# Moving the moment arithmetic of both norms from VectorE to GpSimd

## What is computed

```python
x = x + _L0_conv_ref(_ln_c(x), ...)          # x: (16, 128, 28, 28); norm over the 128 channels of each pixel
t = _to_tokens(x)                            # 12544 tokens of 128 channels
t = t + _L0_ffn_ref(_ln_t(t), ...)           # norm over the channels again, 8 experts, 1024 tokens each

def _ln_c(v, eps=1e-06):
    m = jnp.mean(v, axis=1, keepdims=True)
    s = jnp.var(v, axis=1, keepdims=True)
    return (v - m) / jnp.sqrt(s + eps)
```

## Time and profile before

| what | us |
|---|---|
| median of 3 runs | 503.83 |
| lowest and highest run | 503.77, 505.05 |
| span of the profiled execution | 502.9 |
| busy in it: PE, DVE, ACT, POOL | 361.9, 327.1, 274.3, 159.3 |

### The profile page before, as it was taken

How to read it: one execution, slowest core, us unless ns; L and a number is a source line. 1 busy time by engine, 2 the same in 40 slices (tenths; PEclk the granted TensorE clock), 3 DMA queues, 4 the chain that set the end, 5 groups by cost and what they waited for, 6 DMA issues and landing times. The chain is left out here.

```text
span 502.9 us, 6936 instructions
## 1 busy us (share of the span) xinstructions
PE 361.9 (72%) x1947; PEld 255.7 (51%) x1947; DVE 327.1 (65%) x1004; ACT 274.3 (55%) x587; POOL 159.3 (32%) x151
## 2 busy tenths in 40 slices
PE   4989888888889985631021798999990498876575
PEld 3656555566666553520011374677560467464453
DVE  5699988888889898578879548556620025235444
ACT  3577888888888876677640528556551240510000
POOL 4000000000000000000005777787888788876000
PEclk9999999999999997655555799999997598997755
DMA  4604555555554342479101223344443267847998
GB/s 103 188 38 141 185 168 185 167 185 168 185 182 150 130 131 96 137 238 392 71 1 33 55 56 94 95 65 64 83 85 34 55 189 134 194 61 169 285 390 344
DMA packets 36396, 72.01 MB, mean 143 GB/s; under 512 B 6385, under 2 KB 16785, under 8 KB 36369
## 3 DMA queue, kind: packets, MB, share of 16 engines
q1 hardware_dynamic: 24256, 56.52, 35.0%
q0 software_dynamic: 9472, 8.66, 11.2%
q10 hardware_dynamic: 2640, 6.51, 3.3%
HBM read 34.96 MB, written 30.29 MB: 130 GB/s over the span
## 5 line engine op out<-in xcount | busy, mean ns | idle before, releaser
L403 POOL DMA_INDIRECT picked<-token_rows,slot_idx x32 | 31.5, 986 | 270.7 <-issue 270.4
L691 PE MATMUL psC<-x_pad,tap_diag 128*128 128x392 f32 x256 | 90.8, 498 | 6.7 <-ACT x_pad L570 5.6
L1009 DVE SCALAR_TENSOR_TENSOR conv<-x_pad,taps_w,conv 128x784 f32<-128x784 f32 x64 | 65.9, 1030 | 0.8
L691 PEld LDWEIGHTS psC<-x_pad,tap_diag 128*128 128x128 f32 x256 | 46.1, 189 | 37.0 <-DVE conv L1009 5.1
L1302 DVE TENSOR_TENSOR y_sum<-psC,b_rows 128x512 f32<-128x512 f32 x15 | 10.4, 692 | 75.2 <-PE psC L869 75.2
L869 PE MATMUL psC<-w,hid 128*128 128x128 f32 x480 | 56.6, 280 | 2.2 <-ACT hid L633 2.1
L869 PEld LDWEIGHTS psC<-w,hid 128*128 128x128 f32 x480 | 55.8, 197 | 4.6 <-issue 3.0
L613 ACT ACTIVATE picked_T<-psA 128x512 f32<-128x512 f32 x16 | 9.0, 594 | 59.9 <-PE psA L836 59.9
L426 POOL DMA_INDIRECT moe_sum_late<-y_rows,slot_idx x24 | 37.9, 1581 | 9.5 <-issue 7.0
L483 ACT ACTIVATE rows<-psD,sm 112x128 f32<-112x128 f32 x98 | 35.7, 464 | 9.3 <-DVE sm L1001 9.3
L729 PE MATMUL psB<-act,pw_masked 128*128 128x392 f32 x64 | 27.9, 563 | 17.0 <-DVE pw_masked L1085 17.0
(11 more groups left out here) (211 smaller groups left out, 728.8 us busy)
## 6 DMA issues: line engine op xcount, KB each, us to landing
token_rows<-rows SPq DMA_DIRECT2D x16, 416.5 KB, 3.6
x_in<-in_x_dram SPq DMA_DIRECT2D x16, 392.0 KB, 3.5
x_res<-in_x_dram SPq DMA_DIRECT2D x16, 392.0 KB, 4.3
moe_sum<-zero_rows SPq DMA_DIRECT2D x16, 392.0 KB, 4.9
x_all<-x SPq DMA_DIRECT2D x16, 392.0 KB, 2.9
moe_sum_late<-zero_rows SPq DMA_DIRECT2D x16, 392.0 KB, 7.7
out_dram<-act ACTq DMA_DIRECT2D x16, 392.0 KB, 6.2
w<-in_L_ffn_W_dram SPq DMA_DIRECT2D x16, 256.0 KB, 3.3
```

What stands on the lines that cost most here:

```text
L403: nc.gpsimd.indirect_dma_start(out=picked_in[k][:, b, :], out_offset=None, in_=rows_dram, in_offset=bass.IndirectOffsetOnAxis(ap=slot_idx[ ...
L691: ins = nc.tensor.matmul(psC[:, h, 0:HALF].rearrange("c (h w) -> c h w", w=W), tap_diag[:, n, :], x_pad_v[:, q, y0:y0 + LINES, dx:dx + W], ...
L1009: return nc.vector.scalar_tensor_tensor(o, x_pad_v[:, q, y0 + dy:y0 + dy + lines, dx:dx + W], taps_w[:, PE_TAPS + n:PE_TAPS + n + 1], acc, ...
```

## The change

The five DVE operations go. In their place POOL runs six small `tensor_tensor` operations on the same `st` and `sm`: difference, sum of squares and sum of means, then a square, a product with C/4 out of a small constant tile (`quarter`, set by one more memset), and the addition. Each of the last three waits for a semaphore that the one before it raises. POOL gets its own walk through the 22 steps. DVE's statistics wait for `moments` of the step before, since POOL must have read `st` first.

```diff
+            nc.gpsimd.memset(quarter[:, :], C / 4.0)
...
+            def moments(ln, row, number):
+
+                cols = columns(ln is not None, row is not None)
+                if ln is not None:
+                    pool.wait_ge(s_m1, ln + 1)
+                if row is not None:
+                    pool.wait_ge(s_m3, row + 1)
+                nc.gpsimd.tensor_tensor(sm[:, 1, cols], st[:, cols, 1], st[:, cols, 4], ALU.subtract)
+                nc.gpsimd.tensor_tensor(sm[:, 2, cols], st[:, cols, 2], st[:, cols, 5], ALU.add)
+                nc.gpsimd.tensor_tensor(sm[:, 0, cols], st[:, cols, 1], st[:, cols, 4], ALU.add).then_inc(s_ma, 1)
+                pool.wait_ge(s_ma, number + 1)
+                nc.gpsimd.tensor_tensor(sm[:, 1, cols], sm[:, 1, cols], sm[:, 1, cols], ALU.mult).then_inc(s_mb, 1)
+                pool.wait_ge(s_mb, number + 1)
+                nc.gpsimd.tensor_tensor(sm[:, 1, cols], sm[:, 1, cols], quarter[:, cols], ALU.mult).then_inc(s_mw, 1)
+                pool.wait_ge(s_mw, number + 1)
+                nc.gpsimd.tensor_tensor(sm[:, 3, cols], sm[:, 1, cols], sm[:, 2, cols], ALU.add).then_inc(s_mom, 1)
...
-            def stats(region, lo, s_math, img, s_turned):
+            def stats(region, lo, s_math, img, s_turned, done):
+                if since(done, 1):
+                    dve.wait_ge(s_mom, done)
...
                 if onN:
-                    stats(ln_region(imgN), 0, s_m1, imgN, s_t1)
-                    moments_a(new_ln, new_row, new)
-                    if not on1:
-                        moments_b(img0 + 1, new)
-                        moments_c(img0 + 1, new)
+                    stats(ln_region(imgN), 0, s_m1, imgN, s_t1, img0 + 1)
                 if on1:
                     first_tap(img1, q1, 0)
-                    if onN:
-                        moments_b(img0 + 1, new)
                 if on3:
                     keep_second()
-                if onN and on1:
-                    moments_c(img0 + 1, new)
                 if on3:
                     residual_sum()
                 if on4 and not onN:
-                    stats(row_region(img4), TPI, s_m3, img4, s_t3)
-                    moments_a(None, img4, new)
+                    stats(row_region(img4), TPI, s_m3, img4, s_t3, img0 + 1)
                 if on1:
                     first_tap(img1, q1, 1)
-                if on4 and not onN:
-                    moments_b(img0 + 1, new)
-                    moments_c(img0 + 1, new)
```

More of the change, by code:

```diff
@@ L142, in build @@
         st = sb("st", [P, 2 * TPI, 6])
+        quarter = sb("quarter", [P, 2 * TPI])
         sm = sb("sm", [P, 7, 2 * TPI])
@@ L214, in build, with columns @@
         row_tiles = psD[0:P, :, :].rearrange("p a (t c) -> p (a t) c", c=C)
+        def columns(on_ln, on_row):
+            return slice(0 if on_ln else TPI, 2 * TPI if on_row else TPI)
         def ln_region(img):
@@ L393, in _, with step @@
                            allow_small_or_imprecise_dtypes=True).then_inc(s_const, 1)
+            def moments(ln, row, number):
[13 more added lines that the diff above has]
+                nc.gpsimd.tensor_tensor(sm[:, 3, cols], sm[:, 1, cols], sm[:, 2, cols], ALU.add).then_inc(s_mom, 1)
+            def step(pair, u):
+                onN, imgN, _, _ = image(pair, u, -1)
+                on4, img4, _, _ = image(pair, u, 4)
+                if onN or on4:
+                    moments(imgN if onN else None, img4 if on4 else None, pair * 2 + u + 1)
+            moments(0, None, 0)
+            steps(pool, step)
             def gather(e, half):
@@ L965, in stats @@
                 ins.then_inc(s_math, 1)
-            def columns(on_ln, on_row):
-                return slice(0 if on_ln else TPI, 2 * TPI if on_row else TPI)
-            def moments_a(ln, row, cols):
-                if ln is not None:
-                    dve.wait_ge(s_m1, ln + 1)
-                if row is not None:
-                    dve.wait_ge(s_m3, row + 1)
-                nc.vector.tensor_tensor(sm[:, 1, cols], st[:, cols, 1], st[:, cols, 4], ALU.subtract)
-                nc.vector.tensor_tensor(sm[:, 2, cols], st[:, cols, 2], st[:, cols, 5], ALU.add)
-                nc.vector.tensor_tensor(sm[:, 0, cols], st[:, cols, 1], st[:, cols, 4], ALU.add).then_inc(s_ma, 1)
-            def moments_b(number, cols):
-                dve.wait_ge(s_ma, number + 1)
-                nc.vector.scalar_tensor_tensor(sm[:, 1, cols], sm[:, 1, cols], C / 4.0, sm[:, 1, cols], ALU.mult, ALU.mult)\
-                    .then_inc(s_mb, 1)
-            def moments_c(number, cols):
-                dve.wait_ge(s_mb, number + 1)
-                nc.vector.tensor_tensor(sm[:, 3, cols], sm[:, 1, cols], sm[:, 2, cols], ALU.add).then_inc(s_mom, 1)
             def inverse(ln, row, cols):
@@ L1089, in step @@
                 now_ln, now_row = img0 if on0 else None, img5 if on5 else None
-                new = columns(onN, on4)
-                new_ln, new_row = imgN if onN else None, img4 if on4 else None
                 def keep_second():
@@ L1157, in step @@
                 if on4 and not onN:
[L1158 to L1159 removed]
+                    stats(row_region(img4), TPI, s_m3, img4, s_t3, img0 + 1)
                 if on1:
                     first_tap(img1, q1, 1)
[L1162 to L1169 removed]
+            stats(ln_region(0), 0, s_m1, 0, s_t1, 0)
             setup_first()
```

6 lines of the change are left out of this document (1 added, 5 removed).

## The result

| | before | changed |
|---|---|---|
| median of six runs each, us | 504.63 | 512.15 |
| lowest and highest, us | 503.77, 505.05 | 511.05, 513.59 |
| ratio, 95% interval | | 1.0144 (1.0115 to 1.0173) |
| span of the profiled execution, us | 502.9 | 511.8 |
| mean granted TensorE clock in it | 0.857 | 0.832 |

The change makes the kernel slower by 7.5 us by the medians, 8.9 us by the two profiled spans; the profiled execution of the changed kernel is the longest of its six. The forecast was 507.4 us, with a range of 501.2 to 517.0. The granted clock is given as a share of 2.4 GHz, so that 0.50 in a stretch is the lower level, 1.2 GHz.

The account below looks back on a forecast made before the run. A loop of DVE's mask, PE's products and DVE's statistics to reciprocal, with ACT's roots, was taken as the bound. Full steps -1.8, filling +2.05, draining +3.3 gave +3.6 us: span 506.5, plus 0.9, 507.4 us; range 501.2 to 517.0.

Parts of the forecast that it names:

- What DVE saves: Looped step on DVE: removing the moment operations saves 0.37 us, so DVE alone reaches the reciprocal at T + 2.45.
- T: The end of the last statistics of a step on DVE; in the looped step before, the reciprocal started at T + 2.82.
- X: Time from T to the moments through POOL's six operations, priced by the `affine_select` row: 2.04 us.
- Hold-up by the residual sum: Rival, chance 0.23: POOL's fourth or fifth operation waits for DVE's residual sum; X 2.58 or 3.02 us, total 515 us.
- A full step: Looped step: reciprocal at T + 2.60 instead of T + 2.82, a gain of 0.22 us; eight steps, 1.8 us less.
- the quick rival's case: Rival, chance 0.12: POOL is quick, X 1.48 us, DVE's 0.37 us are had in full in the loop; 501.9 us.
- From the moments to the reciprocal: ACT's roots between moments and reciprocal: 0.37 us with one root, 0.56 us with two, as in a full step.
- Filling: First steps: image 0 loses 1.27 us, image 3 0.78 us, images 1, 2 and 4 nothing; together 2.05 us more.
- Draining: Last steps, token norm only: 0.86, 0.87, -0.69, 1.27 and 1.00 us from first to fifth; together 3.3 us more.

Follow-up runs that it names:

- short-chain run: The changed kernel with POOL's chain cut to its first three operations, so the variance is only a stand-in; 498.36 us, ratio 0.987.
- the one with the sum on DVE: Changed kernel with filling and draining moments on DVE, POOL's chain in two strands, lower half's first tap earlier, sum of means on DVE; 499.58 us, ratio 0.989.
- that pair: The kernel before and the changed kernel, each with 34 unread matmuls added on PE in two draining steps; 507.37 and 508.88 us.
- the kernel before with the early tap: The kernel before with the lower half's first tap moved ahead of the residual sum in full steps; 505.56 us, ratio 0.9999.

## Why the prediction was right and wrong

The direction was right and the time lies in the range, but that it lies there is partly luck: the sum of +3.6 us is half of what was measured, two of its terms have the wrong sign or no counterpart once the clock is kept apart, and the largest part of the loss stands in no term.

1. **What DVE saves.** Right in kind, a little low. Forecast T + 2.45, measured T + 2.39, and T + 2.32 in the short-chain run, where DVE waits for nothing. `moments_c` gave nothing, as forecast: from `keep_second` to the residual sum it is 0.40 us in both kernels (131.98 to 132.38). What was low is `moments_a`. The tap had started at T + 0.33 and now starts at T - 0.09 (131.46), 0.42 us earlier and not 0.29, so that the residual sum starts at T + 0.83, where the forecast put it at T + 0.97.
2. **X, the price of POOL's chain.** Mis-sized in both directions. The nearest row, `affine_select`, was too dear as a price for a wait: a dependent operation follows after 0.07 to 0.08 us (132.07 + 0.23 to 132.37), not 0.25, and the chain alone is 1.61 us, not 2.04; with 7 columns 1.45. The start-to-start distance was 0.18 us, not 0.14. By the estimate from the Trainium skill's page "GPSIMD Engine Reference", section 3.1, an operation would be 0.09 us; it is 0.20 to 0.23 us, and the measurement decides. X = 1.54 us, which that estimate gave, is nearer to the unheld chain only because two errors cancel.
3. **The rival that came true.** Hold-up by the residual sum, which I gave 0.23, is there in all 11 full steps. Its size was smaller than forecast, X = 2.22 with the fifth held against 2.58, since the chain is quicker and the fifth operation started 0.28 us into the residual sum; with the fourth held, in the step at 47 us, X = 2.30 against 3.02.
4. **A full step.** Forecast -0.22 us, measured +0.04 (95.98 - 95.68 over eight), with the reciprocal at T + 2.78 and T + 2.85 in turn, because 2.04 became 2.22. Without the hold-up it would have been 1.61 + 0.56 = T + 2.17, covered by DVE, and -0.43 us, which is the quick rival's case; the short-chain run shows this gain (0.50 us per step), and so does the one with the sum on DVE.
5. **From the moments to the reciprocal.** 0.37 and 0.56 us, as forecast.
6. **Filling.** The two terms were 1.27 and 0.78; the chains themselves lost 0.68 (T + 1.82 against T + 1.14) and 0.19 us (30.19 is T + 1.82, against T + 1.63). Image 1, which I had put at 0, lost 0.69 us on its own chain (T + 1.82 against T + 1.13), and all of it was on the path, since DVE stood idle for it; with the moments of filling back on DVE the distance from image 0 to image 1 was 6.08 us, as before (6.04), and not 6.77. These three make 1.56 us. Image 2 gave 0.35 us back (6.90 us behind image 1, against 7.25), and T of image 0 lay 0.15 us earlier. Measured in all: +1.3, not +2.05.
7. **Draining.** This is the step that was furthest off. +3.6 measured against +3.3 forecast is a coincidence: with the clock kept up in both kernels the changed one drained 0.6 us faster (47.2 against 47.8). Term by term, in that pair: the first +0.3 for 0.86, the second +0.6 (12.09 to 12.69) for 0.87, the third -0.9 for -0.69, the last +0.4 for 1.00. The fourth chain grew by 0.68 us and not 1.27, and nothing of it reached the next reciprocal: from the 19th to the 20th it is 7.54 us after 7.74 in the first two profiles, and 6.70 after 7.72 in the pair. What filled the sum is a term that was missing.
8. **TensorE's clock.** The missing term. With the earlier fall the way from the 17th to the 18th reciprocal grew by 4.1 us; the run with filling and draining on DVE and the two with added matmuls show that most of this does not come from the chain. The +3.2 us behind the search, where no instruction differs, were not in the forecast either. They differ from execution to execution, whoever makes the moments: 246.9 us in the profile of the kernel before with the early tap, which makes no moment on POOL, and 242.6 us in the changed kernel with added matmuls, which has all of them. The granted clock differs with them (from 262 to 300 us 0.71 before, 0.60 changed and 0.68 with added matmuls; beyond 300 us 0.86, 0.83 and 0.86). Two things stay open. All six executions of the changed kernel took 511 us or more, and none of the kernel before in any batch took more than 508.2; whether the change itself makes the early fall more likely no run shows. And the mean clock alone does not fix the time: at 0.842 the changed kernel took 511.05 us and the kernel before, in a later batch, 507.26.

So the loss between the two profiled executions is, as far as the runs separate it: about 1.3 us in filling, the longer chains; 0.5 us in the full steps, where the hold-up takes back a gain of over 3 us; and the larger part, in draining and behind the search, with the clock, which fell earlier.

## What to carry to other kernels

Moving small work to GpSimd pays only where the wait for its result is covered by other work: price the whole chain with its hand-overs, here 1.6 us for six operations, against the cover that is really there. Then look at which DVE operations with two SBUF inputs start just ahead of one of GpSimd's, because each of those can add up to its own length; one more DVE operation of 0.1 us in between was worth 3.5 us here, though the hold-up came back in one step of 11. A gain or loss of a few us in one stage can be outweighed by where TensorE's clock falls, so compare stages before totals.

## What was not expected of the hardware

- GpSimd's dependent operations cost only 0.07 us for the wait, and the first started 0.15 us after DVE's last statistics. The operation itself is 0.20 us with 7 elements and 0.23 us with 14.
- A DVE operation with one input of 784 32-bit elements from SBUF (`tensor_scalar`, 0.6 us) also stretches GpSimd's, to 0.55 to 0.59 us. The page "SBUF — State Buffer" of the Trainium skill, in "Who interferes with whom", counts `tensor_scalar` among the operations that can take the shared ports, and the trace agrees.
- The hold-up is decided within 0.1 us, and the recorded starts don't settle it. The addition 0.02 us behind the residual sum took 1.07 us; started 0.06 to 0.09 us ahead, it took 0.22 to 0.24 us in seven steps of the loop and 1.18 us in the eighth, and where it was quick it cost the residual sum nothing that shows (1.02 to 1.03 us). In the changed kernel the fourth operation of one looped step started 0.02 us behind the residual sum (72.37 and 72.35) and took 0.21 us.
- The clock's first fall moved by 5.5 us between two kernels whose PE had been busy alike for 37 us up to 184 and 182 us. In the one it fell while PE worked, in the other while PE waited.
